# Five GpSimd drains in the expert stage of a MetaFormer block with a top-2 mixture of experts

## The reference, cut to what matters

```python
x = x + conv_mixer(layernorm_c(x))                 # gates, 3x3 depthwise conv, rfft2 feature
t = to_tokens(x)                                    # 2048 tokens of 256
xt = layernorm(t)
S = sigmoid(xt @ Wg)                                # 8 experts
G, I = top_k(S, 2)
h = gelu(einsum('nd,edf->enf', xt, W1) + b1)        # 256 -> 1024
y = einsum('enf,efd->end', h, W2) + b2              # 1024 -> 256
out = sum over the token's two experts of G * y
x = from_tokens(t + out)
```

## Time and profile before

| | |
|---|---|
| median of three runs | 341.78 us |
| span of the profiled execution | 341.7 us |
| PE busy | 305.1 us, 89% |
| DVE busy | 249.4 us, 73% |
| ACT busy | 182.0 us, 53% |
| POOL busy | 153.3 us, 45% |
| indirect adds to `out` (L530) | 39, mean 1604 ns on GpSimd |
| indirect gathers (L520) | 39, mean 1261 ns on GpSimd |

### The profile page before, as it was taken

One profiled execution on the slowest core, in us unless ns is written; L12 is line 12 of the kernel. 1 busy time (PEld: TensorE's weight loads), 2 busy tenths in 40 slices (PEclk: granted clock), 3 DMA queues, 4 the chain that ended last, 5 costly groups with the idle time before them and its releaser, 6 DMA issues.

```text
span 341.7 us, 8716 instructions
## 1 busy us (share of the span) xinstructions
PE 305.1 (89%) x3066; PEld 231.2 (68%) x3066; DVE 249.4 (73%) x596; ACT 182.0 (53%) x509; POOL 153.3 (45%) x162
## 2 busy tenths in 40 slices
PE   8999899999610788999999999999999999999960
PEld 8777633567410386888888888888888888877730
DVE  3896978669899689979797978888756564665430
ACT  3547487616723355676767676666534445354310
POOL 2233542347520630665655554665455453635331
PEclk9999999999965699999999999999999999999995
DMA  7500000002379383788787878784353433333210
GB/s 215 171 3 1 2 0 1 0 31 88 115 238 287 87 269 109 213 207 215 199 198 196 204 196 197 195 206 79 67 87 62 87 63 69 64 56 64 52 19 2
DMA packets 36202, 39.42 MB, mean 115 GB/s; under 512 B 8416, under 2 KB 32832, under 8 KB 36160
## 3 DMA queue, kind: packets, MB, share of 16 engines
q1 hardware_dynamic: 29184, 29.56, 29.2%
q0 software_dynamic: 6976, 9.31, 16.1%
HBM read 29.74 MB, written 9.11 MB: 114 GB/s over the span
## 4 chain that ended last, share of the span: by engine, by line
PE 67%; DVE 14%; DMA 10%; issue 3%; ACT 2%; POOLq 0%; POOL 0%; SPq 0%; ACTq 0%
PE ps L912 15%; PE ps L897 8%; PE ps L901 8%; PE ps L899 8%; DMA out<-fb,idx 8%; PE ps L913 8%; PE ps L756 5%; PE ps L737 3%; DMA xt<-x_tok 2%; PE ps L851 2%; PE ps L765 2%; PE ps L769 2%; PE ps L772 2%; PE ps L845 2%; PE ps L804 1%
## 5 line engine op out<-in xcount | busy, mean ns | idle before, releaser
L674 ACT ACTIVATE fb<-ps,b1t 128x128 f32<-128x128 f32 (+7 forms) x312 | 82.0, 376 | 83.6 <-issue 80.8
L912 PE MATMUL ps<-wt,fb 128*128 x312 | 117.0, 379 | 0.0
L897 PE MATMUL ps<-fb,wt 128*128 128x128 f16 (+7 forms) x624 | 114.3, 214 | 2.7 <-DVE fb L1357 2.7
L901 PE MATMUL ps<-fb,wt 128*128 128x128 f16 (+7 forms) x624 | 114.3, 214 | 0.9 <-issue 0.9
L899 PE MATMUL ps<-fb,wt 128*128 128x128 f16 (+7 forms) x624 | 114.3, 214 | 0.0
L530 POOL DMA_INDIRECT out<-fb,idx x39 | 62.6, 1604 | 96.4 <-DVE s2c L1400 62.6
L913 PE MATMUL ps<-wt,fb 128*128 x312 | 85.0, 272 | 0.0
L897 PEld LDWEIGHTS ps<-fb,wt 128*128 x624 | 61.0, 98 | 33.6 <-issue 3.8
L899 PEld LDWEIGHTS ps<-fb,wt 128*128 x624 | 60.4, 98 | 3.3
L520 POOL DMA_INDIRECT fb<-xn_rows,idx x39 | 49.2, 1261 | 26.3 <-DVE idx L1335 12.8
L901 PEld LDWEIGHTS ps<-fb,wt 128*128 x624 | 60.4, 98 | 0.4 <-issue 0.4
(11 more groups left out here) (209 smaller groups left out, 397.1 us busy)
## 6 DMA issues: line engine op xcount, KB each, us to landing
wt<-w SPq DMA_DIRECT2D x32, 512.0 KB
b2t<-b SPq DMA_DIRECT2D x39, 128.0 KB
out<-xt SPq DMA_DIRECT2D x8, 256.0 KB, 2.1
xn_rows<-wt SPq DMA_DIRECT2D x8, 256.0 KB, 3.3
xt<-x_tok SPq DMA_DIRECT2D x3, 512.0 KB, 6.9
b1t<-params SPq DMA_DIRECT2D x39, 4.0 KB
fb<-xn_rows,idx POOLq DMA_INDIRECT x39
out<-fb,idx POOLq DMA_INDIRECT x39
```

Source lines behind the costliest of these rows:

```text
L674: a = nc.scalar.activation(hid[:, s, f * P:f * P + ROWS[n]], h_ps(s)[:, f * P:f * P + ROWS[n]], ACT.Gelu_apprx_tanh, bias=b1t[:, n % NBIAS ...
L897: pe.matmul(dst, hi, xT[:, s, c * P:c * P + rows], start=(c == 0 and f % 4 == 0), stop=False, skip_group_check=True)
L901: m = pe.matmul(dst, lo, xT[:, s, c * P:c * P + rows], start=False, stop=(c == DC - 1), skip_group_check=True)
L912: pe.matmul(y_ps(s), hhi[:, s, f * P:(f + 1) * P], w, start=(f == 0), stop=False)
```

## The change

In `add`, at i = 6, 12, 18, 24 and 30, GpSimd executes a drain between the wait for the landing of add i - 1 and the wait for the result of tile i. A drain holds the engine's queue until older instructions are complete. No other instruction is added or removed, and none changes its place on any engine. From line 85 on, the line numbers of the changed kernel are larger by one, and behind the drain by three.

```diff
@@ -82,6 +82,7 @@
 DVE_GATES = 13
 POOL_PADS = 6
+RETIRE = range(6, TILES - 6, 6)
 
@@ -526,6 +527,8 @@
 
                 if i > 0:
                     pool.wait_ge(add_out, 16 * i)
+                if i in RETIRE:
+                    pool.drain()
                 pool.wait_ge(y_done, i + 1)
                 nc.gpsimd.indirect_dma_start(
```

## The result

The changed kernel takes 339.70 us (median of 22 runs), the kernel before 341.88 us (22 runs beside it). The ratio is 0.993, 95% interval 0.9915 to 0.9945, which is 1.9 to 2.9 us less. The forecast was 337.4 us, 4.3 less. The profiled execution had a span of 337.0 us at a run time of 338.89, so 1.9 us lie around a span, which I had taken for nothing. By that, the median run of the kernel before has a span of about 340.0 us, and its profiled execution, with 341.7, was a long one.

A forecast was written before the change was run, and what follows sets the result against it. PE was taken to bound the kernel until about 299.5 us, then a serial string of adds ending in GpSimd's last drain. Sum: 341.7 - 4.4 + 0.1 = 337.4 us, range 336.5 to 341.9.

The forecast's parts named there:

- rival A: GpSimd's drains clear DMA entries one by one, so early drains shorten the last: 337.4 us, own range 336.5 to 339.5; chance 0.80.
- rival B: Last drain does work of the program's end that early drains don't take over: no change, 341.7 us; chance 0.10.
- Term 1: Last GpSimd drain: 67 of 78 entries already cleared at 0.065 us each, 4.4 us less; upper end 5.0, lower end nothing.
- Term 2: Drain ahead of add 30, the only one on the string to the end: loss 0.1 us, up to 0.8.
- Whatever delays add 30 delays the end by as much: Adds of tiles 30 to 38 are one serial string, so a delay of add 30 reaches the end in full.
- Term 3: Drains ahead of adds 6, 12, 18 and 24: delay gone within two adds, price 0; without cover a tenth or two each.
- PE's stretch up to 299.5 the same in each case: Sign for all cases: PE's part of the chain, up to 299.5 us, stays the same to a tenth of a microsecond.
- adds 7, 13, 19 and 25 stand where they stood: Sign of being right: these adds, which follow the adds behind the first four new drains, keep their places.
- the string begins within 0.3 us of 301.30: Sign of being right: the string of adds from add 30 on starts within 0.3 us of its old start.
- Rival C: Every drain with DMAs behind it costs a fixed 5.1 us; add 30 is 4.1 us late: 345.8 us; chance 0.10.
- a new drain lasts over 2.5 us and add 30 starts after 303: Sign that the forecast is wrong and each drain has a fixed price; add 30 started at 301.30 before.

The follow-up runs named there:

- e1_only30: Against the kernel before, one early drain only, ahead of add 30, where it finds 67 uncleared DMAs; ratio 0.9948.
- e9_order_behind: Against the kernel before, five drains behind the wait for the previous add's landing, with gather i + 6 issued behind add i; ratio 0.9962.
- e2_only6: Against the kernel before, one early drain only, ahead of add 6, with 19 entries; ratio 0.9979.

## Why the prediction was right, and where its sizes were off

The mechanism of the saving was right. The size was not: 339.70 us lies above A's own range (336.5 to 339.5) and inside the whole one (to 341.9) only because that had been carried on to cover half of rival B, which is luck and not foresight.

- *Entries cleared one by one* (rival A, 0.80): right. 12, 19, 59, 67 and 78 entries take 1.02, 1.54, 4.8, 5.54 and 6.5 us of clearing: 0.081 to 0.085 us each. I took 0.065, counting from the landing; the upper end of the term, 0.083 from the end of descriptor writing, was the true one. The three figures of line 107 and rows 5 fit both, and only a second count (59 or 67) told them apart. The kernel before also had long drains at its end on the other engines (0.52 us on DVE, 1.24 on ACT, 2.41 on PE), where I had called them short; they end before 332 us and aren't on the path.
- *Term 1, the last drain, -4.4*: measured -4.45, in part by luck. With 0.083 us an entry the term says 5.0; but the drain also ends 0.45 us behind the landing when all old entries can have been cleared under the flight, and that tail was in no term.
- *Term 2, add 30 late by 0.1 (up to 0.8)*: the drain itself, 1.17 us (I had 0.79 to 1.0), and the 0.76 us of issue behind it (0.75) were nearly as reckoned. But the cover was gone, because add 29 was already 2.9 us late: add 30 stood 4.4 us late against tile 0. The loss at the end was less, 1.6 us, because the string recovers (e1_only30: 6.1 us at add 30, 2.9 at the end). "Whatever delays add 30 delays the end by as much" was wrong: the last nine adds were no serial string, since DVE's results held 34 to 36.
- *Term 3, the drains ahead of adds 6 to 24, priced 0*: this is the term that was mis-sized. I had looked only at whether the next add could start in time with a landing of 5.13 us. The landing itself got longer, 6.86 us for add 6, and the drain at 6 had to wait 2.5 us for gather 12, in a stretch where transfers crowd. The trace of before could have warned: 11 of adds 1 to 20 were released by a landing there, add 6 among them, and not by DVE's result, and the 2.5 us of idle time "in nearly every tile" are found in each tile only from 21 on. Lateness then lasted to the end, each new drain adding to it, and DVE's waits for landings (28.2 us in the whole run, 2.1 before) cost PE 1.84 us by tile 32. (Of that, the waits themselves show 1.3 us more of PE waiting for DVE's rows, 4.0 instead of 2.7; the rest isn't traced to a wait.) Part of that time comes back at the end of the string: the last add is 1.6 us late.
- *PE's stretch up to 299.5 the same in each case*: wrong, for the same reason. So are the signs that adds 7, 13, 19 and 25 stand where they stood (they are 4.7, 6.0, 5.3 and 7.5 us late) and that the string begins within 0.3 us of 301.30.
- *Rival B*, no effect, and the two rules of the Trainium skill behind it (the short constant DRAIN; the drain that waits for its engine to go idle): the first doesn't fit GpSimd's drains here, 1.02 to 9.97 us. The second holds as far as it goes, since every last drain here ended behind the last landing, but it leaves the clearing out.
- *Rival C*, a fixed price: refuted by 5.54 us for 67 entries against 1.02 for 12. Yet its sign, "a new drain lasts over 2.5 us and add 30 starts after 303", came true (4.08 us, and 303.88). It was badly chosen: a drain that waits for a gather gives it too.

The saving was forecast well and its cost was not: the sum, 4.3 us against 2.4 measured, is off by 1.9, and the lateness is 1.6 us at the last add in the profile.

One more thing shows in the late gathers: writing their descriptors takes GpSimd 1.48 us in the mean and not 1.26. An example, a gather of 1.74 us where the kernel before has one of 1.10 (GpSimd, and DVE beside it):

```profile
252.87 1.74 POOL L521 DMA_INDIRECT fb<-xn_rows,idx  x1 [0.30 <-issue]
```

```profile
252.52 1.22 DVE L1390 SCALAR_TENSOR_TENSOR fb<-fb 128x1024 f16<-128x1024 f32 x1
```

DVE's operation ends at 253.74, 0.87 us after the gather began, and the gather needs another 0.87 from there. Before, the gather of 254.03 began 0.25 us before the end of the same operation (253.05 + 1.23 = 254.28) and took 0.25 + 0.85. Of the gathers in both traces up to 270 us, those that begin inside one such operation of DVE (two inputs in SBUF, 1.2 us) take what is left of it and 0.85 to 0.88 us more, in the kernel before too; what changed is how much is left. The Trainium skill, SBUF — State Buffer, section Who interferes with whom, says that a Vector instruction with two SBUF inputs contends with a GpSimd instruction that reads SBUF, and that such contention is an exclusive lock and no sharing. These rows agree in their numbers, if a gather counts as such an instruction (it reads `idx`); no run here took DVE's operation away.

## What to carry to other kernels

Look at what GpSimd's last drain does behind the last landing: with 78 indirect DMAs it was 5.1 us on the path, and early drains take that time off the end. Put such a drain where the only transfer in flight is one that the engine waits for anyway, with nothing else queued ahead of it, and move the gather that would stand there behind the add. In this form even a stretch where the DMA engines are nearly full cost nothing that can be measured (0.9875, against 0.9869 and 0.9878 with the drains elsewhere); behind the wait the same drains gained less (0.993, 0.9962). A wait of a microsecond that the next step seems to absorb must be checked against the landing time that the shifted transfer will have, not the one it had.

## What the runs showed of the hardware

- A GpSimd drain takes 0.081 to 0.085 us for each indirect DMA issued since the last one (12, 19, 59, 67, 78 of them). It counts DMAs and not their rows: 12 entries of which four had 64 to 112 rows took 1.02 us, like 12 of 128 rows (e9_order_behind).
- It works on old ones while the newest is in flight, but ends only when all have landed, gathers included (4.08 us with a gather in flight, 5.05 in e2_only6, and 1.54 us without, 19 entries each).
- The add behind a drain started 0.76 us after its end, as behind DVE's result (0.75); behind a landing it is 0.27 us.
- The writing of a gather's descriptors on GpSimd that begins inside a two-input operation of DVE takes the rest of that operation and 0.85 to 0.88 us more (0.87 + 0.87 and 0.25 + 0.85 us in the two examples).
- A 3.54 us fill of SBUF on GpSimd stretched a DVE operation of 0.69 us to 2.86 us.
